# Routed experts of the first layer: token rows scattered into expert tiles in place of every expert on every token

## What is computed

```
shared = new_gelu(xf @ Wfc_s + bfc_s) @ Wproj_s + bproj_s       # 128 -> 512 -> 128
probs = softmax(xf @ Wr); topk_p, topk_i = top_k(probs, 2)       # 2 of 8 experts for each token
gate[token, topk_i] = topk_p / sum(topk_p)                       # 0 for the other six
routed = 0
for e in range(8):
    routed = routed + (new_gelu(xf @ Wfc[e] + bfc[e]) @ Wproj[e] + bproj[e]) * gate[:, e:e + 1]
out = shared + routed
```

## Time and profile before

| what | us |
|---|---|
| median of 3 runs (2334.02 to 2335.99) | 2335.16 |
| the profiled execution | 2343.62 |
| its span, first to last instruction | 2341.9 |
| PE busy | 2097.0 (90%) |
| DVE busy | 1542.6 (66%) |
| ACT busy | 1373.8 (59%) |
| POOL busy | 487.9 (21%) |

### The profile page before, as it was taken

How to read it: one execution, slowest core, us unless ns; L and a number is a source line. 1 busy time by engine, 2 the same in 40 slices (tenths; PEclk the granted TensorE clock), 3 DMA queues, 4 the chain that set the end, 5 groups by cost and what they waited for, 6 DMA issues and landing times. The chain is left out here.

```text
span 2341.9 us, 43593 instructions
## 1 busy us (share of the span) xinstructions
PE 2097.0 (90%) x10732; PEld 1351.8 (58%) x10732; DVE 1542.6 (66%) x6216; ACT 1373.8 (59%) x2513; POOL 487.9 (21%) x808
## 2 busy tenths in 40 slices
PE   3479999999963999999977999999999997499998
PEld 2245555555533788888733555555555547378886
DVE  4378778877825677777755666666666633567776
ACT  1236666666653889999842555555555565355554
POOL 4101111111103000000000111111111110266665
PEclk9779999999995999999986999999999998599999
DMA  3533334333301221122166555555555521076552
GB/s 95 175 51 54 53 46 60 51 50 50 46 22 63 55 55 37 37 45 45 18 234 186 127 118 117 117 121 128 128 128 117 117 46 58 25 157 120 132 122 60
DMA packets 96650, 202.81 MB, mean 87 GB/s; under 512 B 14496, under 2 KB 32160, under 8 KB 96032
## 3 DMA queue, kind: packets, MB, share of 16 engines
q1 hardware_dynamic: 96544, 201.65, 38.8%
HBM read 169.47 MB, written 31.60 MB: 86 GB/s over the span
## 5 line engine op out<-in xcount | busy, mean ns | idle before, releaser
L575 DVE CUSTOM_DVE_ANT_0 a1ms<-a1S,mask_q 128x128 bf16<-128x128 f32 (+1 forms) x758 | 387.8, 553 | 182.6 <-issue 179.1
L629 ACT ACTIVATE a1p<-a1T 128x512 f32<-128x512 f32 x576 | 331.4, 597 | 293.9 <-PE a1T L731 293.4
L575 DVE CUSTOM_DVE_ANT_0 a0ms<-a0S,mask_q 128x384 bf16<-128x384 f32 (+2 forms) x752 | 379.7, 553 | 109.6 <-issue 108.2
L629 ACT ACTIVATE a0p<-a0T 128x512 f32<-128x512 f32 x576 | 330.0, 597 | 188.7 <-PE a0T L731 177.8
L710 PE MATMUL a1O<-a1p,a1v 128*33 128x512 f32 (+3 forms) x1536 | 304.3, 496 | 1.0 <-POOL a1p L543 0.9
L731 PE MATMUL a0T<-a0qT,a0kT 128*128 128x512 f32 (+3 forms) x768 | 265.4, 392 | 18.3 <-DMA a0qT<-a0mr 6.8
L1184 DVE TENSOR_TENSOR m_hl<-m_h,m_hh 128x512 fp32r<-128x512 f32 x288 | 197.7, 690 | 116.8 <-ACT m_hh L1140 111.7
L731 PE MATMUL a1T<-a1qT,a1kT 97*128 97x512 f32 (+3 forms) x768 | 262.8, 390 | 0.7 <-DMA a1qT<-a1mr 0.7
L670 PE MATMUL a0S<-a0kS,a0qS 128*128 128x384 f32 (+2 forms) x752 | 229.0, 361 | 27.9 <-DMA a0kS<-scr_k 21.7
L731 PEld LDWEIGHTS a1T<-a1qT,a1kT 97*128 97x128 f32 x768 | 131.6, 189 | 200.7 <-ACT a1p L629 144.5
L670 PE MATMUL a1S<-a1kS,a1qS 96*128 96x128 f32 (+1 forms) x758 | 220.6, 353 | 13.0 <-DMA a1kS<-scr_k 12.8
(11 more groups left out here) (234 smaller groups left out, 3628.3 us busy)
## 6 DMA issues: line engine op xcount, KB each, us to landing
m_gb<-scr_g SPq DMA_DIRECT2D x48, 1024.0 KB, 8.6
a1qS<-scr_q SPq DMA_DIRECT2D x96, 256.0 KB, 6.1
a1qT<-scr_q SPq DMA_DIRECT2D x96, 256.0 KB, 4.0
a1kS<-scr_k SPq DMA_DIRECT2D x96, 128.0 KB, 6.8
a1kT<-scr_k SPq DMA_DIRECT2D x96, 128.0 KB, 4.7
scr_q<-p_hi SPq DMA_DIRECT2D x32, 256.0 KB, 2.5
scr_q<-p_lo SPq DMA_DIRECT2D x32, 256.0 KB, 2.7
a0qS<-scr_q SPq DMA_DIRECT2D x48, 128.0 KB
```

What stands on the lines that cost most here:

```text
L575: nc.vector.tensor_tensor_reduce(masked_s[spare][:, 0:c1 - c0], buf[:, 0:c1 - c0], k.mask_q[:, SEQ - w + c0:SEQ - w + c1], 1.0, NEVER, ALU ...
L629: nc.scalar.activation(prob_of(g, p)[:, h, :], t_ps[slot % 2][:, :], ACT.Exp, scale=scale)\
```

## The change

The routed experts no longer run on every token. `route_0` also works out, for each token and each of its two experts, a place in a list of 23 tiles of 512 places. The list is ordered by expert and each expert begins a new tile (8192 pairs fill 16 tiles, and up to 7 more are begun). `experts_0` replaces `moe_0` and has two phases:

- Phase 1: the shared expert on the 8 supertiles (32 steps). Beside it DVE normalises each 128-token tile twice into a ring of 8 buffers, with the gate and the return index behind the 128 values, and POOL scatters each buffer into `slot_rows` in HBM: 64 indirect DMAs of 128 rows of 520 bytes.
- Phase 2: 23 tiles. SP loads a tile into one of 4 buffers `xt`. PE turns it (`turn_x`), ACT and DVE split it, DVE reads the tile's expert into a register and copies that expert's weights to a fixed place, and 4 steps of the same kind as before follow. Then ACT adds the bias (`keep_y`), PE turns the result back (`turn_y`), DVE multiplies it with the gates (`weigh`, into `yo`), and POOL scatters it to `pair_rows` in 4 indirect DMAs of 128 rows of 512 bytes. A place that no pair holds has an index that is out of bounds and is not written.
- At the end SP loads the 8192 pair rows back, and DVE adds them to `x` (16 additions) and takes the statistics.

`slot_rows` is filled beforehand with a padding row, by one DMA of 11776 rows that SP issues inside the first attention (`after_loads`). The gate rows of layer one, their turning and their 32 stores are gone. Several semaphores are shared between blocks, and `route` is split in two functions; the second layer's computation stays.

```diff
+SLOT_TILES = 2 * TOK // ST + 7
+SLOTS = SLOT_TILES * ST
+ROW = D + 2
 def attention(...):
                 for h in range(HG):
                     set_row((0, 0), h)
+                if after_loads is not None:
+                    after_loads(sp)
                 main_steps(sp, step)
+def pad_slots(sp):
+    sp.dma_start(slot_rows.rearrange("(t p) c -> p t c", p=P),
+                 k.pad[:, :].unsqueeze(1).broadcast_to([P, SLOTS // P, ROW])).then_inc(padded, 16)
+def experts_0(...):
+    RING, XBUF, YBUF = 8, 4, 3
+    # SP
+    for s in sent:
+        sp.wait_ge(s, ALL_SENT)
+    for t in range(SLOT_TILES):
+        if t >= XBUF:
+            sp.wait_ge(y_sent[t % XBUF], sent_tiles(t - XBUF))
+        rows = slot_rows[t * ST:(t + 1) * ST, :].rearrange("(p i) c -> p (i c)", i=TPS)
+        sp.dma_start(xt[t % XBUF][:, :, :].rearrange("p i c -> p (i c)"), rows).then_inc(x_loaded[t % XBUF], 16)
+    for t in range(SLOT_TILES - XBUF, SLOT_TILES):
+        sp.wait_ge(y_sent[t % XBUF], sent_tiles(t))
+    # then 16 loads of pair rows, 256 KB each
+    # POOL
+    for q in range(2 * TILES):
+        pool.wait_ge(staged, 2 * (q + 1))
+        nc.gpsimd.indirect_dma_start(slot_rows, ..., stage[q % RING][:, :], None, ...).then_inc(sent[t % (RING // 2)], 16)
+    for t in range(SLOT_TILES):
+        pool.wait_ge(yo_ready, t + 1)
+        for i in range(TPS):
+            nc.gpsimd.indirect_dma_start(pair_rows, ..., yo[t % YBUF][:, i, :], None, ...).then_inc(y_sent[t % XBUF], 16)
+    # PE, phase 2: j is the tile, ch its step
+        if j < j1:
+            fc(n)
+        if NCH * j0 <= n - LAG < NCH * j1:
+            project(n - LAG)
+        if ch == 0 and j0 == NSH and j + 1 < j1:
+            turn_x(j + 1)
+        if ch == 1 and j0 <= j - 2 < j1:
+            turn_y(j - 2)
+    # DVE
+        if j < j1:
+            split(n)
+        if j0 == 0 and n < TILES:
+            send(n)
+        if j0 == NSH and j + 1 < j1:
+            if ch == 0:
+                e = expert_of(j + 1)
+                copy_fc(j + 1, e)
+            if ch == 1:
+                split_x(j + 1)
+            if ch == 3:
+                copy_project(j + 1, e)
+        if ch == 2 and j0 <= j - 2 < j1:
+            (add_shared if j0 == 0 else weigh)(j - 2)
```

More of the change, by code:

```diff
@@ L73, in __init__, with params_loaded @@
         self.x = sb("x", [P, TILES, D], F32)
+        self.pad = sb("pad", [P, ROW], F32)
         self.stats = sb("stats", [P, TILES, 6], F32)
         self.mean, self.rstd, self.tmp = (sb(n, [P, TILES], F32) for n in ("mean", "rstd", "dev"))
+        self.loaded, self.loads = self.sem("k_ld"), 0
+        self.ln_sems = self.sem("ln_comb"), self.sem("ln_std")
+        self.ln_counts = [0, 0]
     def sem(self, name):
         return self.ctx.enter_context(self.nc.semaphore(name))
+    def params_loaded(self, n):
+        self.loads += n
+        return self.loaded, 16 * self.loads
 def causal_pieces():
@@ L107, with ln_stats @@
 NP = len(PIECES)
-def ln_stats(k, name, x_loaded=None):
-    nc, sem = k.nc, k.sem
-    combined, std_ready = sem(name + "_comb"), sem(name + "_std")
+def ln_stats(k, x_loaded=None):
+    nc = k.nc
+    combined, std_ready = k.ln_sems
+    before, before_std = k.ln_counts
+    LINKS = 8 + (TILES if x_loaded is not None else 0)
+    k.ln_counts = [before + LINKS, before_std + 1]
     st = k.stats
@@ L119, in _ @@
         def _(dve):
-            n = [0]
+            n = [before]
             if x_loaded is not None:
@@ L155, in _ @@
         def _(act):
-            act.wait_ge(combined, (TILES if x_loaded is not None else 0) + 7)
+            act.wait_ge(combined, before + LINKS - 1)
             nc.scalar.activation(k.rstd[:, :], k.rstd[:, :], ACT.Sqrt).then_inc(std_ready, 1)
@@ L200, in prepare @@
         if zeroed:
[L202 removed]
+            pool.wait_ge(done, 2 + len(zeroed))
         for t in self.kT:
@@ L320, in back, with attention @@
                     last.then_inc(v_done, 1)
-                pe.wait_ge(loaded, 48)
+                pe.wait_ge(loaded, LOADED)
                 pipelined(pe, NST // 2, front, back)
-def attention(k, name, HG, VD, scale, operands, load_q, load_k, load_v, out, PARTS=1, BURST=1, HALVES=2):
+def attention(k, name, HG, VD, scale, operands, load_q, load_k, load_v, out, after_loads=None,
+              PARTS=1, BURST=1, HALVES=2):
     nc, sem = k.nc, k.sem
@@ L825, in _, with __init__ @@
                         tile_stats(k, dve, g, added)
-def route(k, name, E, K, w_router, bias_row, xh, xl, gate_rows, weights, weights_loaded):
-    nc, sem = k.nc, k.sem
-    PAD = 6 if K == 2 else 0
-    LOADED = 16 if bias_row is None else 32
-    TAKEN, FILL = (-1.0, 3.0) if K == 2 else (-3e38, 0.0)
+class Routed:
+    def __init__(self, nc, c):
+        sb = lambda n, s, d: c.enter_context(nc.sbuf_tensor("rt_" + n, s, d))
+        self.slot = [sb(f"slot{i}", [P, TILES], U32) for i in range(2)]
+        self.extra = sb("extra", [P, TILES, 2, ROW - D], F32)
+        self.expert = sb("expert", [1, SLOT_TILES], I32)
@@ L854, in route @@
         g_ps = [pb(f"g{i}") for i in range(2)]
[L855 to L858, removed]
+        xn_ready, xT_done, xs_ready, xh_ready, xl_ready = (sem(name + n) for n in ("xn", "xT", "xs", "xh", "xl"))
+        loaded, LOADED = k.params_loaded(2)
+        l_done, lg_ready, pr_ready, chain, g_done, g_kept, gt_ready, w_split = (
+            sem(name + n) for n in ("l", "lg", "pr", "ch", "gd", "gk", "gt", "ws"))
         g_stored = [sem(f"{name}gst{i}") for i in range(2)]
@@ L1586, in _ @@
                                     pattern=[[-1, P]], channel_multiplier=1).then_inc(made, 1)
+            nc.gpsimd.memset(k.pad[:, 0:D + 1], 0.0).then_inc(made, 1)
+            nc.gpsimd.memset(k.pad[:, D + 1:ROW].bitcast(U32), SKIPPED).then_inc(made, 1)
 def transformer(nc, a, out):
```

659 lines of the change are left out of this document (452 added, 207 removed).

## The result

The changed kernel takes 2459.23 us (median of 4 runs, 2458.01 to 2459.91) against 2335.57 for the kernel before (median of 4) on the same chip: 1.0513 times, 95% interval 1.049 to 1.0535. A second measurement of the same program, on another occasion, gave 2451.71 us and 1.0468 (1.0433 to 1.0502). The forecast was 2416. The profiled span went from 2341.9 to 2458.2, +116.3 us.

A forecast was written before the change was run, and what follows sets the result against it. PE bounds the experts now; after the change phase 2's chain through four buffers would. Experts +68.1, routing +3.1 and padding +10 make +81 us, a median of 2416 us; range 2295 to 2505.

The forecast's parts named there:

- Phase 2, 19 tiles of 16.9: Routed experts: the four-buffer chain from turn_x to turn_x takes 16.9 us a tile, 321.1 us over 19 tiles.
- (c): Sign to look for in the new profile: the first tiles of phase 2 at 7.5 us.
- Phase 1, 88.4: Shared expert with 64 scatters at POOL's pace: 88.4 us before phase 2's first matmul.
- A scatter at 1.2 us: Each indirect DMA costs POOL 1.2 us, in both phases; each us of that price counts 144 times.
- Rival 1: The scatter is cheap, 0.35 us, so the sum falls by 122 to 2294 us; chance 0.14.
- The clock, 2.2 us a tile: Phase 2: PE idles and its clock falls, so a tile takes 16.9 us cold against 14.7 warm.
- Rival 4: The clock stays up although PE idles in phase 2: 42 us less, 2374 us; chance 0.10.
- The tail: End of the experts: last scatters 4.8 + 1.6 us, then pair loads 2.3 + 20.3 and last addition and statistics 2.5.
- Routing +3.1: Routing stage: 32 stores go, DVE gets about 28 small instructions, so the experts start 3.1 us later.
- Padding +10: First attention: the padding DMA delays group 2's loads, so PE waits 10 us once.
- Rival 3: DVE and POOL ports collide (phase 1 38 us, phase 2 28 us more: 2482) or scatters cost 1.9 us (2517); chance 0.14.
- The forecast's 171 us: Experts: PE's matmul time given for the fall from 288 steps to 124.

The follow-up runs named there:

- e1: Six xt buffers instead of four, otherwise the changed kernel; 2248.38 us, 0.960 of the kernel before the change.
- e10: Changed kernel with two of each tile's four phase 2 scatters left out and the padding stored late; 2394.96 us, 1.0226 of the kernel before.
- e11: Changed kernel (four xt buffers) with 34 useless matmuls ahead of turn_x from the fifth tile on; 2421.86 us, 1.0337 of the kernel before.
- e12: Five xt buffers instead of four, otherwise the changed kernel; 2287.69 us, 0.9779 of the kernel before.
- e7: Changed kernel with six xt buffers and the padding issued after the queue's last attention step; 2232.29 us, 0.9552 of the kernel before.
- e9: The changed kernel itself measured again, nothing edited; 2451.71 us, 1.0468 of the kernel before.

## Why the prediction was right, and where its sizes were off

The time fell into the range, on the expected side, by the expected mechanism. It was 43 us under the measured median. Point by point:

**Phase 2, 19 tiles of 16.9: right.** Measured 17.30 on the mean, 17.04 in the tile shown, whose parts err both ways: `turn_x` to `weigh` 7.16 (8.0), the hand-over to POOL 0.78 (0.2), scatters 5.22 (4.8), landing and load 3.88 (3.9; the landing 1.1 and not 1.6, the load 2.8 and not 2.3). From phase 2's first `fc` to the end of the last `weigh` the trace has 360.1 us, the forecast 357.4: the 19 tiles are 7.6 us longer than forecast, what stands before and behind them 4.9 shorter. e1, e10, e11 and e12 show that the ring, the scatters and PE's part are all in this chain. The first tiles ran at 4 to 6.5 us (7.5), with buffers loaded ahead, as (c) said.

**Phase 1, 88.4: too short by 20.** The trace has 108.4 (777.01 to 885.45). ACT's stops are about 11 of it by e7, which is the term that was missing. The rest is in e7's 97.0 us. The 64 scatters take 1.32 us each with the waits among them, 84.2 in all (76.8), the first starts 6.4 us into the stage (5.3), landing and load behind them take 3.9 (3.9), and turning and splitting 2.6 (2.4).

**A scatter at 1.2 us: near.** 0.97 of execution and 0.30 between two, 1.275 us in a dense row. Rival 1 (0.35) is out. The slope was too steep: I took each us of scatter as a us of period, and e10's two scatters fewer take 2.54 us out of their part of the chain, but only 1.96 out of the period, since the clock came back later.

**The clock, 2.2 us a tile: too much.** It falls, as said: the two matmuls that follow `turn_x` start 0.43 us apart or more, and phase 2's clock is 0.77 on the mean. But the warm chain is 15.8, not 14.7 (e11). The warm estimate for PE's and ACT's part, 5.8, was right (5.81). The cold one was too long by 0.8, and hand-over and scatters too short by 1.0. The forecast of 16.9 held because these two cancel. That is luck. Rival 4's price would have been 30 us, not 42.

**The tail: 3.4 us too short.** Behind the end of the last `weigh` the trace has 34.9 us, the forecast 31.5. POOL falls behind once the buffers are no longer waited for: the last three `weigh` start within 4.2 us, and their twelve scatters queue. The last scatter ends 11.6 us behind the last `weigh`, where I had 4.8. The pairs' loads and additions take 22.2 (25.1). The timeline of the tail:

```profile
1244.82 0.69 DVE L1336 TENSOR_TENSOR m_yo<-m_yT,m_xt 128x512 f32<-128x512 f32 x1 [1.44 <-PE m_yT L1227]
...
1256.10 0.97 POOL L1162 DMA_INDIRECT scr_pairs<-m_yo,m_xt  x1 [0.30 <-issue]
...
1258.29 0.38 SPq L1147 DMA_DIRECT2D xh<-scr_pairs  x1
```

**Routing +3.1: measured +3.0. Padding +10: +12.4** in the profiled execution, by the mechanism named, 6 to 13 in the first attention over the ten profiles with it.

**The rest.** +6.7 us in stages whose work is unchanged. It is there in the profiles of all twelve runs behind it too, as +2.5 to +9.1; PE's busy time is the same to 0.3 us (1078.63 against 1078.36); its cause wasn't sought. And I put the median below the profiled time, as it was before the change, while the changed kernel's profiled run was at its median: another 7.8 us. With 26.1 from the experts and 2.4 from the padding these make up the 43 us.

**Rival 3, the ports.** A scatter takes 0.97 us alone, about 1.18 when it starts beside DVE's weight copies, and mostly 0.97 beside the normalisations and subtractions of phase 1 (1.01 on the mean of those 64); the longest has 1.56. The mean of phase 2's 92 is 1.064, by the group of the profile:

```profile
L1162 POOL DMA_INDIRECT scr_pairs<-m_yo,m_xt x92 | 97.9, 1064 | 280.5 <-DVE m_yo L1336 257.9
```

That is 9 us of issue in phase 2 in all, not 28, and 3 in phase 1, not 38. The Trainium skill, "SBUF — State Buffer", section "SBUF: two separate sides", has the port pair of DVE and GpSimd as an exclusive lock; these rows agree with it in direction, and a block for the whole of each DVE instruction isn't seen. The Trainium skill, "DMA: Bandwidth & Descriptors", section "Anatomy of one DMA — SWDGE (gpsimd) path", gives a fixed 2.0 us for a DMA of GpSimd, setup and completion together. The trace agrees: the scatters of e7's phase 1 land 2.3 us after they start, at the median. But 0.97 of these are POOL's own time, which my sum had already. Behind it 1.3 us are left, less than my 1.6, so to put 2.0 there, as the forecast's last sentence on the skill does, would have counted a part twice.

**Where the time of the matmuls went.** The forecast's 171 us are the 124 steps that stay (124 x 1.38); the 164 steps that go are 226 us. PE's busy time fell by 156 of them, since part of what stays runs at the lower clock. And PE's idle time in front of `turn_x` in phase 2 is 172 us, more than the busy time fell. With six buffers there is none in phase 2, and the gain is there: 2248, and 2232 with the late padding.

## What to carry to other kernels

Count the tiles between the last read of a buffer and the first need of its next content, and set the length of the return path (here 9.9 us: scatter, land, load) against as many tiles of work. With one tile between, the period was PE's part plus the return path (17.3 us); with two, about half of that (8.8); with three, PE's own pace (6.45). A cheap-looking software scatter belongs in that sum at its full 1.3 us each, and so does the clock that falls while the engine waits.

Before rejecting a change that removes work and comes out slower, try the count of its buffers. Two buffers of 2 KB a partition were the difference between 5% slower and 4% faster.

## What the runs showed of the hardware, unexpected

- Beside a dense row of indirect scatters on POOL (one per 1.3 us, 128 rows of 520 bytes) ACT stood 2 to 10 us at a time, 30 to 44 us in all within some 105, with its inputs ready and no releaser. Scatters of 512-byte rows in phase 2, 4 per 6.4 us in e1, stopped nothing. On one of four occasions (four programs on one chip) it didn't happen at all. What ACT waits for isn't shown.
- An indirect scatter of 128 rows costs POOL 0.97 us and 0.30 to the next, whether 520 or 512 bytes a row, and 1.18 beside DVE's weight copies (1.56 at most).
- Filling PE's idle 9 us with matmuls of no use made the kernel 30 us faster (e11 against e9): the granted clock of phase 2 was 0.99, not 0.77, and the transposes and matmuls behind each wait ran at 2.4 GHz, not 1.2.
- With half of the scatters (e10) the chain's scatters fell by 2.5 us a tile and the period by only 2.0: in every second tile the granted clock stayed at about 0.50 through the first 6 us, and that part took 8.4 us and not 7.5.
